# Batch 0 of an attention and feed-forward kernel: the k projections of batch 1 move ahead of the branch on inexact weights, the turn of the first normalized tokens behind it

## The reference

```python
q, k, v = x @ Wq.T + bq, x @ Wk.T + bk, x @ Wv.T + bv      # 16 heads of 16
p = softmax(q @ k.T / sqrt(512)) * triu(ones)
x1 = layernorm(x + p @ v) * gamma + beta
x2 = layernorm(x + x1)
h = silu(lin(x2, w1)) * lin(x2, w2)
h = gelu(lin(h, h1))
h = gelu(lin(h, h2))
out = layernorm(x2 + lin(h, w3))
```

## Time and profile before

| | |
|---|---|
| median of 3 runs | 1188.02 us (1187.51 to 1189.85) |
| profiled execution, span from first to last instruction | 1187.2 us (the page gives no other time for it) |
| PE busy | 1149.0 us, 97% of the span |
| DVE, ACT, POOL busy | 784.1, 492.9, 401.8 us |
| chain that ended last, by engine | PE 93%, DVE 4%, DMA 1%, ACT 1%, issue 1% |
| mean granted clock of PE | 0.977 |

### The profile page before, as it was taken

How to read it: one execution, slowest core, us unless ns; L and a number is a source line. 1 busy time by engine, 2 the same in 40 slices (tenths; PEclk the granted TensorE clock), 3 DMA queues, 4 the chain that set the end, 5 groups by cost and what they waited for, 6 DMA issues and landing times.

```text
span 1187.2 us, 18377 instructions
## 1 busy us (share of the span) xinstructions
PE 1149.0 (97%) x7311; PEld 809.2 (68%) x7311; DVE 784.1 (66%) x1276; ACT 492.9 (42%) x660; POOL 401.8 (34%) x373
## 2 busy tenths in 40 slices
PE   6499999999999999999999999999999999999997
PEld 3255778667785777757777577866778577775886
DVE  5986773778737776487755777377873777648513
ACT  4475312762138511574117631276213751156311
POOL 1343423144222632235222352315332262212432
PEclk8589999999999999999999999999999999999999
DMA  8971332422224422323244133242222432232000
GB/s 303 338 208 59 112 82 56 108 97 82 73 55 109 142 69 53 87 67 141 72 91 108 55 120 78 55 108 105 74 73 56 109 142 71 48 69 68 1 1 18
DMA packets 44954, 111.71 MB, mean 94 GB/s; under 512 B 8000, under 2 KB 19648, under 8 KB 44864
## 3 DMA queue, kind: packets, MB, share of 16 engines
q1 hardware_dynamic: 40016, 98.01, 29.2%
q10 hardware_dynamic: 4848, 12.47, 3.1%
HBM read 88.95 MB, written 21.50 MB: 93 GB/s over the span
## 4 chain that ended last, share of the span: by engine, by line
PE 93%; DVE 4%; DMA 1%; ACT 1%; issue 1%; POOL 0%; SPq 0%; POOLq 0%; ACTq 0%
PE PS L1244 54%; PE PS L1156 11%; PE PS L1180 7%; PE PS L1120 6%; PE PS L1063 5%; PE PS L1187 3%; PE PS L1193 2%; DVE neg_max L784 2%; PE PS L1080 2%; DMA stacks<-qk_rows 1%; ACT probsT L678 1%; PE PS L1209 1%; PE PS L1344 1%; DMA qk_rows<-qk_lo 0%; PE PS L1288 0%
## 5 line engine op out<-in xcount | busy, mean ns | idle before, releaser
L777 DVE TENSOR_REDUCE neg_max<-PS 128x3 f32<-128x1536 f32 (+1 forms) x168 | 256.9, 1574 | 61.9 <-PE PS L1120 61.9
L540 POOL TENSOR_TENSOR hidA_lo<-hidA_full,hidA_hi 128x512 fp32r<-128x512 f32 x128 | 174.1, 1360 | 225.6 <-DVE hidA_hi L1024 180.5
L678 ACT ACTIVATE probsT<-PS 128x1024 f32<-128x1024 f32 x192 | 184.6, 1023 | 53.4 <-PE PS L1156 49.3
L1244 PE MATMUL PS<-hidA_hi,g 128*128 128x512 f32 x512 | 205.5, 401 | 0.4 <-POOL hidA_lo L540 0.4
L1244 PE MATMUL PS<-hidC_hi,g 128*128 128x512 f32 x512 | 203.0, 397 | 0.0
L1244 PE MATMUL PS<-hidA_lo,g 128*128 128x512 f32 x512 | 199.9, 391 | 0.0
L1244 PE MATMUL PS<-hidC_lo,g 128*128 128x512 f32 x512 | 199.7, 390 | 0.0
L540 POOL TENSOR_TENSOR hidC_lo<-hidC_full,hidC_hi 128x512 fp32r<-128x512 f32 x64 | 82.2, 1285 | 202.0 <-DVE hidC_hi L1024 202.0
L1156 PE MATMUL PS<-stacks 66*128 66x512 f32 x512 | 147.3, 418 | 1.6 <-DVE neg_max L784 1.1
L699 ACT ACTIVATE hidC_full<-PS,scales 128x512 f32<-128x512 f32 x64 | 44.2, 690 | 243.1 <-PE PS L1244 243.1
L699 ACT ACTIVATE hidA_full<-PS,scales 128x512 f32<-128x512 f32 x64 | 44.1, 689 | 218.6 <-PE PS L1244 218.6
(11 more groups left out here) (131 smaller groups left out, 1650.4 us busy)
## 6 DMA issues: line engine op xcount, KB each, us to landing
stacks<-qk_rows SPq DMA_DIRECT2D x124, 256.0 KB
stacks<-qk_rows SPq DMA_DIRECT2D x246, 128.0 KB
qk_rows<-qk_hi SPq DMA_DIRECT2D x16, 512.0 KB, 2.7
qk_rows<-qk_lo SPq DMA_DIRECT2D x16, 512.0 KB, 2.9
xT_sb<-xT_dram SPq DMA_DIRECT2D x8, 512.0 KB, 4.0
g_raw<-h1T_dram ACTq DMA_DIRECT2D x4, 1024.0 KB, 12.1
g_raw<-h2T_dram ACTq DMA_DIRECT2D x4, 1024.0 KB, 16.7
x_tok<-x_dram SPq DMA_DIRECT2D x8, 512.0 KB, 5.0
```

The costliest lines, as they stand in the source:

```text
L540: nc.gpsimd.tensor_tensor(lo[:, m, :], full[:, m, :], hi[:, m, :], ALU.subtract).then_inc(lo_done, 1)
L678: nc.scalar.activation(probs(s)[:, 2 * pair:2 * pair + 2, :], PS[:, bank:bank + 2, :], ACT.Exp, scale=SCALE).then_inc(exp_done, 1)
L777: ins = nc.vector.tensor_reduce(NEGM[:, half, at:at + hi - lo], PS[:, bank:bank + hi - lo, :], AX.X, ALU.max, negate=True)
L1244: ins = nc.tensor.matmul(out, d if swapped else w, w if swapped else d, start=(k == 0 and part == 0), stop=(k == kts - 1 and part == 1))
```

## The change

In batch 0 alone, the k projections of batch 1 (8 PE instructions with their weight loads) go to the end of `attention(0)`, ahead of the branch; the turn of part 0 stays behind the branch and so now comes after them. ACT's list for batch 0 follows: all four biases first, then both parts of x2T_hi. Batches 1 to 7 are as before, and so is the amount of work.

```diff
                 if not last:
-                    bias_qk(b + 1, range(DT))
+                    bias_qk(b + 1, range(2 * DT if first else DT))
                 take_x2_hi(b, 0)
-                if not last:
+                if not first and not last:
                     bias_qk(b + 1, range(DT, 2 * DT))
                 take_x2_hi(b, 1)
...
                 if b < B - 1:
                     project_half(b + 1, 1, 1)
+                if b == 0:
+                    project(b + 1, range(DT, 2 * DT))
                 return inexact
...
                 turn_x2(b, 0, last)
                 if not last:
-                    project(b + 1, range(DT, 2 * DT))
+                    if b:
+                        project(b + 1, range(DT, 2 * DT))
                     project_v(b + 1, range(QT // 2))
```

## The result

Over 21 runs each, the kernel after takes 1186.04 us in the median (1184.96 to 1188.27) and the kernel before 1188.16 (1186.80 to 1189.93). The ratio is 0.9985, 95% interval 0.9979 to 0.9991: the change is faster by 1.1 to 2.5 us. The forecast was 1184.2. That is 0.15% less, where 0.32% was forecast. The profiled execution of after has a span of 1183.4 us, the very number forecast for the span, and took 1185.42 us.

A forecast was written before the change was run, and what follows sets the result against it. PE, busy 97% of the 1187.2 us span, was taken as the bound; 0 (work) - 1.91 (idle) - 1.87 (clock) = -3.78 us gave span 1183.4, median 1184.2 us; main case 1183.0 to 1185.6, stated range up to 1187.4.

The forecast's parts named there:

- step 1: PE, batch 0's branch: k projections of batch 1 ahead of it hide the 1.91 us idle; gain 1.91 us.
- B: At PE's branch: it waits for the array, so the idle only moves behind the k projections; 1188.0 us, 15%.
- step 2: PE's clock behind the idle: without that idle it never drops to half; gain 1.87 us, bounds 0 and 1.87.
- The yardstick of batch 1: Last q projection to feed-forward: 8.54 us in branchless batch 1, 12.32 in batch 0; excess 3.78 us.
- A: The main forecast: idle and clock loss both go, median 1184.2 us, range 1183.0 to 1185.6; 68%.
- the stated range: Range for the measured median, up through C to 1187.4 us, leaving out B and Rival D, 0.2 together.
- C: At PE's branch: idle partly hidden or clock dips all the same, one term returns; 1186.1 us, 12%.
- The base of the sum: Starting time for the forecast: profiled span 1187.2 us, taken as 0.8 us under the median of 1188.02.
- steps 3 to 5: Six transposes 0.66 us at full clock; ScalarE's k biases before x2T_hi, cost 0; earlier GpSimd parts and k store, 0.
- Rival D: At PE's branch: its instruction fetch meets the q store's DMA traffic; slower, 1189.3 to 1190.6 us, 5%.

The follow-up runs named there:

- the drained kernel: The changed kernel plus a PE wait for the last k projection to finish before the branch; ratio 1.0026, median 1192.37 us.
- the repeat of after: The changed kernel, unedited, profiled once more; span 1186.8 us against 1183.4 in its first profile.
- the second profile of before: The kernel before, unedited, profiled once more; idle ahead of the transposes but no fall of the clock; span 1185.1 us.

## Why the prediction was right, and where it was not

*The idle (step 1).* Right, with its reason. PE's sequencer reaches the branch while its array has work, and the branch's 3.6 us pass beside it. The estimate of where it was reached, 104.3, stands against 105.16 - 1.0 = 104.1 by the drained kernel. The rival in which the idle only moves (B) is what the drained kernel shows, and only because a wait forces it. The Trainium skill's queue of 64 instructions (page "TensorE: Matmul & The Clock Gate", specification table) is contradicted by no run here; none shows where the queue would be full. The Trainium skill's 108 ns for a compare-and-branch (page "Advanced Engine Details and Errata", Control Flow Timing) is a thirtieth of what this branch took; for this branch the measured 3.58 us decides.

*The clock (step 2).* This is the step that failed. "I take 1.87" treated the dip of one profile as a property of the kernel. It was in one of four profiles of before; an average run pays about a quarter of it by that count. The size was off too: of the 1.87 us, 0.19 is lost at full clock as well (transposes 0.85 against 0.66), and the dip itself cost 1.7. Idle of 1.65 us (the mean of 1.91, 1.64, 1.45 and 1.59), 0.19 and a quarter of 1.7 give 2.3 us, and the runs' means differ by 1.9 (1188.38 and 1186.47): four profiles are few, and the runs leave less room for dips than a quarter. The yardstick of batch 1 was sound; what it measured was one execution. The forecast's condition on the clock ("no such idle is left") did hold: neither profile of after has a dip behind 100 us.

*What was luck.* The span forecast, 1183.4, was met to the digit because the two profiles compared were alike in their start (low stretch to 70.2 and 70.4 us, the same group of DVE at 46.45 and 46.24) and the one of before had the rare dip. Against the repeat of after, 1186.8, the same change would have shown 0.4 us, and against the second profile of before 1.7. The measured median of 1186.04 lies outside the 1183.0 to 1185.6 that the prediction gives for A; it is inside the stated range because that was drawn up through C. And the outcome that got 0.67, faster by over 0.2%, didn't come: 0.15% is below the 0.2% that the prediction took as the least change that can be told, though 21 runs of each kernel do tell it.

*The base of the sum.* The span of 1187.2 was set 0.8 us under the median of 1188.02. Every later run lists both, and a run takes 1.7 to 2.1 us more than its span (1185.42 and 1183.4; 1187.10 and 1185.1). The profiled execution had thus taken about 1189.2, above the median by 1.2. Its dip and this are one and the same error, and 1183.4 + 2.0 - the forecast's 1184.2 = 1.2 us is the part of it that stayed in the median forecast.

*The turn, ScalarE, GpSimd, the stores (steps 3 to 5).* Transposes 0.66 us as forecast. ScalarE's last bias ended at 110.44 (110.5 forecast), DVE was done at 112.61, and the margin was 0.5 us, not 0.2. The low parts ended at 114.72 (forecast 114.9). The k store was issued near 110.8 and nobody waited for it. Rival D, the fetch that meets the stores, didn't come: the packet moved 2.3 us before SP even issued the first of them.

Rival C (one of the two terms comes back) had named the time that was measured, 1186.1, for the wrong reason: the dip did not appear after the change, it was mostly missing before it.

What is open: what decides when the low stretch of the start ends (69.1 to 76.6 us in the profiles), and why the first profile had a dip and its three repeats none. The Trainium skill, page "TensorE: Matmul & The Clock Gate" (Part 1), says that the activity monitor runs free of the kernel's start and that the transition therefore varies from run to run. The ends listed here do vary, but by 7.5 us, and no run here could set that phase, so whether it is the reason isn't shown.

## What to carry to other kernels

A branch on PE is hidden if the array has as much queued work as the branch takes, here 3.6 us, from the point where the sequencer can reach it; so put independent matmuls ahead of it and no wait between them and it. Set the span of a profile against the median only through a run that lists both, and before a clock dip goes into a sum, look at a second profile: it may belong to one execution. Edits that fill PE's pauses must stay under the engine that sets the pace, or they become the pace.

## What the hardware showed that was not expected

- This taken branch on PE cost 3.58 us from an empty array to the next matmul (one profile): 1.0 us until its instruction packet moves and 2.55 from there to the first work, 2.5 to 2.8 in the four profiles of before and 2.95 in the kernel before with throw-away matmuls.
- PE's clock fell behind an idle of 1.91 us in one run and behind one of 3.58 us, but not behind idles of 1.45, 1.59, 1.64 and 1.80 us at the same place.
- The flag's pause of 0.44 us cost 0.71 us of the chain, all at full clock: with the pause gone, the four q instructions around it take 1.91 us in place of 2.62.
- The low stretch at the start ended anywhere from 69.1 to 76.6 us and the start's loads landed up to 1.0 us apart; together they made 3.4 us between two executions of one program (2.4 and 1.0), about as much as the runs spread.
